# A decoder layer on one core: the clip of the weight preparation as one instruction, and mixing's inputs loaded in seven pieces

## The chip, the cores and the metric

The kernel runs on 1 core of one Trainium2 chip. The metric is the device time of one execution in microseconds (us). TensorE is called PE, VectorE DVE, ScalarE ACT, GpSimd POOL and SyncE SP, as the profile does. SP computes nothing here; it issues nearly all DMAs, in the order in which they are written, and stands still at each of its waits.

## The reference, cut to what matters

The layer takes x (16 x 128 x 256) through three parts with a layer norm behind each: a two-way RWKV mixing (`_L0_attn_ref`), a cross attention to `ctx_1024` with 16 heads, and a block of causal attention with 8 experts, two of them per token. The weights of the last block are quantised and dequantised in groups of 128 values before use:

```
w2 = w.reshape(-1, 128)
wmax, wmin = max(w2), min(w2)
scales = clip(wmax - wmin, 1e-5, None) / 15
base = clip(round(-wmin / scales), 0, 15)
wq = (clip(round(w2 / scales) + base, 0, 15) - base) * scales
```

The change is in the code that computes these lines for the attention weights and the experts' down projections.

## The kernel before, in words

The program is a list of stages (`STAGES`): prep, mix, cross, attend, route, experts, finish. Every engine has one stream of instructions that runs through the stages in order; semaphores order the engines among each other. So an engine that is done with its part of prep may start its part of mix, if what that waits for is there.

**Prep** works on 11 jobs (`NUMBERS`). A job is 128 partitions of 14 groups of 128 f32 values (`TILES` = 14, `P` = 128), 896 KB. Three buffers each of `raw`, `level`, `turned` and `stat` rotate (index j = n mod 3). For job n:

- SP loads it from `weight_jobs` into `raw` (L312).
- DVE reduces each group to its maximum and minimum (L261, L262) and computes the small numbers, 14 a partition, in eight steps that each wait for the one before (`group_steps`, L263 to L271): scale, inverse, base, and `LOW`/`HIGH`, the ends between which the rounded value is to be clipped.
- ACT rounds: 14 instructions (L372), one a group, each adding MAGIC = 1.5 x 2^23, so that f32 rounds to whole numbers.
- DVE clips groups 0 to 9 in ten instructions (L358), POOL clips groups 10 to 13 in four (L398), both between `LOW` and `HIGH` of the group.
- POOL dequantises: 14 instructions (L405), (level - MAGIC) x scale.
- PE transposes the 14 tiles into four banks (L422), ACT copies the banks to `turned` (L381), SP stores them to `numbers_d` (L317), from where later stages load them.

The order on each engine is written out: DVE does the numbers of job n+1 and then clips job n; ACT rounds job n+2 and then copies job n; POOL and PE take the jobs in turn. The numbers of job n+1 wait until POOL has dequantised job n-2, whose `stat` buffer they take (semaphore `dequantised`). SP's order: loads of jobs 0, 1, 2; then, each behind the rounding of an earlier job that frees its buffer, the loads of jobs 3 and 4; then all inputs of mixing (`load_mix_inputs`: `w_rkv`, two `x_turned`, `w_out`, `decay`, `first`, and the first `x_group`, about 6.5 MB) and of cross (`load_cross_weights`, seven DMAs, about 1 MB); then for n from 2 on: wait for the rounding of job n, load job n+3, wait for the copies of job n-2, store it.

**Mix** starts on DVE, ACT and POOL when SP has seen the last store of prep land and raises `begun` (L173), and on PE when the last bank of prep is copied and the mixing inputs are there (`mix_loads`, 16 a DMA, `LOADS` = 6 of them). PE projects (L527), ACT takes the result (L573). SP's part begins with the loads for attend (L214 to L218) and goes on with the next group of x (L186) when DVE has the variances of the group before.

**Cross** has a preparation of its own for 16 more jobs, interleaved with attention. It finds the small numbers with `group_range` and `group_bias` (L232 to L252: sums over pairs made with `tensor_reduce`, through a buffer with a gap of one, `spaced`), adds `BIAS` = base + MAGIC when rounding (L1056), clips the whole job in one instruction between MAGIC and MAGIC + 15 (L1199), and subtracts `BIAS` on POOL in two halves with the `BIAS` of each group broadcast along its 128 values (L1128).

Of the kernel before, what the change touches and what calls it, by code (L numbers as in the profile page):

```python
# [22 lines left out]
ALU = mybir.AluOpType  # L23
# [3 lines left out]
P = 128  # L27
# [14 lines left out]
TILES = 14  # L42
# [53 lines left out]
class Shared:  # L96
# [75 lines left out]

        sp.sem_inc(self.begun, 1)  # L173

    def load_mix_inputs(self, sp):
        t = self.t
        for src, dst in ((t["rkv_t"], self.w_rkv), (t["x_fwd_t"], self.x_turned[0]), (t["x_bwd_t"], self.x_turned[1]),
                         (t["out_t"], self.w_out)):
            sp.dma_start(dst[:, :, :], src.rearrange("(c p) n -> p c n", p=P)).then_inc(self.mix_loads, 16)

        sp.dma_start(self.decay[:, :], t["decay"]).then_inc(self.mix_loads, 16)
        sp.dma_start(self.first[:, :], t["first"]).then_inc(self.mix_loads, 16)
        self.load_group(sp, 0)
# [46 lines left out]
def group_range(dve, st, a, groups):  # L230

    dve.tensor_reduce(a[:, MAX, :], groups, AX.X, ALU.max)  # L232
    st.did(dve.tensor_reduce(a[:, NEG_MIN, :], groups, AX.X, ALU.min, negate=True))  # L233
# [18 lines left out]
    return dve.tensor_reduce(in_pairs(BIAS), row_pair(a, BASE, SHIFT), AX.X, ALU.add)  # L252


def group_steps(dve, st, a, groups):

    def step(ins):
        st.did(ins)
        st.wait()

    dve.tensor_reduce(a[:, MAX, :], groups, AX.X, ALU.max)  # L261
    step(dve.tensor_reduce(a[:, MIN, :], groups, AX.X, ALU.min))  # L262
    step(dve.tensor_tensor(a[:, TMP, :], a[:, MAX, :], a[:, MIN, :], ALU.subtract))  # L263
    step(dve.tensor_scalar(a[:, SCALE, :], a[:, TMP, :], 1e-5, 1.0 / LEVELS, ALU.max, ALU.mult))
    step(dve.reciprocal(a[:, INV, :], a[:, SCALE, :]))
    step(dve.scalar_tensor_tensor(out=a[:, TMP, :], in0=a[:, MIN, :], scalar=-1.0, in1=a[:, INV, :],
                                  op0=ALU.mult, op1=ALU.mult))
    step(dve.tensor_scalar(a[:, BASE, :], a[:, TMP, :], MAGIC, MAGIC, ALU.add, ALU.subtract))
    step(dve.tensor_scalar(a[:, TMP, :], a[:, BASE, :], 0.0, LEVELS, ALU.max, ALU.min))
    step(dve.tensor_scalar(a[:, LOW, :], a[:, TMP, :], -1.0, MAGIC, ALU.mult, ALU.add))  # L270
    return dve.tensor_scalar(a[:, HIGH, :], a[:, LOW, :], LEVELS, None, ALU.add)  # L271


def prep_stage(k):


# [4 lines left out]
    with ExitStack() as own:  # L281
        raw = [k.buffer(own, f"raw{j}", [TILES, P]) for j in range(3)]
        level = [k.buffer(own, f"level{j}", [TILES, P]) for j in range(3)]
        turned = [k.buffer(own, f"turned{j}", [TILES, P]) for j in range(3)]
        stat = [k.buffer(own, f"stat{j}", [8, TILES]) for j in range(3)]
    raw_in = [k.semaphore(f"raw_in{j}") for j in range(3)]
    stored = [k.semaphore(f"stored{j}") for j in range(3)]
    scale_ready = k.semaphore("scale_ready")
    rounded = k.semaphore("rounded")
    clipped = k.semaphore("clipped")  # L290
    pool_clipped = k.semaphore("pool_clipped")
# [4 lines left out]
    DVE_TILES = 10  # L296
# [12 lines left out]

    def sync(sp):  # L310
        def load(j, n):
            sp.dma_start(raw[j][:, :, :], t["weight_jobs"][bass.ds(n, 1)].rearrange(  # L312
                "o p (a b) -> (o p) a b", a=TILES)).then_inc(raw_in[j], 16)

        def store(j, n):
            sp.wait_ge(bank_read, (n + 2) * BANKS_JOB)
            sp.dma_start(k.numbers_d[bass.ds(n, 1)].rearrange("o p (a b) -> (o p) a b", a=TILES),  # L317
                         turned[j][:, :, :]).then_inc(stored[j], 16)

        def element(j, n, more=True, begin=False):  # L320

            if more:
                sp.wait_ge(rounded, n + 1)
                load(j, n + 3)
            if not begin:
                store((j + 1) % 3, n - 2)

        for j in range(3):
            load(j, j)
            sp.sem_inc(stored[j], 16)  # L330
        for n in range(2):
            element(n, n, begin=True)
        k.load_mix_inputs(sp)
        k.load_cross_weights(sp)
        with sp.Fori(0, TURNS) as i:
            for d in range(3):
                element((2 + d) % 3, 3 * i + 2 + d)
        for n in range(3 * TURNS + 2, NUMBERS):
            element(n % 3, n, more=False)
        for n in range(NUMBERS - 2, NUMBERS):  # L340
            store(n % 3, n)
        for j in range(3):
            sp.wait_ge(stored[j], 16 * (1 + len(range(j, NUMBERS, 3))))

    def vector(dve):
        st = k.steps["dve"]

        def steps_of(j, n, i):
            dve.wait_ge(raw_in[j], 16 * i + 16)
            dve.wait_ge(dequantised, n + 1)  # L350
            group_steps(dve, st, stat[j], raw[j][:, :, :]).then_inc(scale_ready, 1)

        def element(j, n, i, more):
            if more:
                steps_of((j + 1) % 3, n + 1, i + (j + 1) // 3)
            dve.wait_ge(rounded, n + 1)
            for a in range(DVE_TILES):
                last = dve.tensor_scalar(level[j][:, a, :], level[j][:, a, :], stat[j][:, LOW, a:a + 1],  # L358
                                         stat[j][:, HIGH, a:a + 1], ALU.max, ALU.min)
            last.then_inc(clipped, 1)  # L360

        dve.tensor_copy(k.ident16[:, :], k.ident).then_inc(k.s_fill, 1)
        steps_of(0, 0, 0)
        st.done(1, 8)
        in_pipeline(element, dve, st, 24)
        st.done(1, st.at)

    def scalar(act):
        def round_levels(j, n):
            act.wait_ge(scale_ready, n + 1)  # L370
            for a in range(TILES):
                last = act.activation(level[j][:, a, :], raw[j][:, a, :], ACT.Identity, bias=k.magic[:, :],  # L372
                                      scale=stat[j][:, INV, a:a + 1])
            last.then_inc(rounded, 1)

        def take_tiles(j, n, i):
            act.wait_ge(stored[j], 16 * i + 16)
# [12 lines left out]
        round_levels(1, 1)  # L390
        in_pipeline(element, act)

    def gpsimd(pool):
        def element(j, n, i, more):
            pool.wait_ge(rounded, n + 1)
            pool.sem_inc(k.s_held, 1)
            for a in range(DVE_TILES, TILES):
                last = pool.tensor_scalar(level[j][:, a, :], level[j][:, a, :], stat[j][:, LOW, a:a + 1],  # L398
                                          stat[j][:, HIGH, a:a + 1], ALU.max, ALU.min)
            last.then_inc(pool_clipped, 1)  # L400
            pool.wait_ge(clipped, n + 1)
            pool.wait_ge(pool_clipped, n + 1)
            pool.sem_inc(k.s_held, 1)
            for a in range(TILES):
                last = pool.tensor_scalar(level[j][:, a, :], level[j][:, a, :], -MAGIC,  # L405
                                          stat[j][:, SCALE, a:a + 1], ALU.add, ALU.mult)
            last.then_inc(dequantised, 1)

        pool.sem_inc(dequantised, 3)
        in_pipeline(element, pool)  # L410

    def tensor(pe):
        def element(j, n, i, more):
# [17 lines left out]
def mix_stage(k):  # L431
# [6 lines left out]
    nc, t, banks = k.nc, k.t, k.banks  # L438
    x_turned, w_rkv, w_out = k.x_turned, k.w_rkv, k.w_out
    decay, first, x_group, group_in = k.decay, k.first, k.x_group, k.group_in  # L440
    LOADS = 6
    with ExitStack() as own:
        step_decay = k.buffer(own, "step_decay", [UNITS])
        top = [k.buffer(own, f"top{p}", [GB, S + 1]) for p in range(2)]
# [47 lines left out]
    def sync(sp):  # L492
# [8 lines left out]
        k.begin(sp, "mix")  # L501
        sp.sem_inc(mix_stored, 16)
        k.load_attend_weights(sp)
        with sp.Fori(0, GROUPS - 1) as g:
            element(g, True)
        sp.wait_ge(mix_stored, 32)
# [1873 lines left out]
```

## Time and profile before

| | us |
|---|---|
| median of 3 runs | 1266.79 |
| lowest, highest | 1266.73, 1269.02 |
| profiled execution | 1267.29 |
| its span | 1265.5 |
| prep: the first raw reduction to the last copy | 8.7 to 123.2 |
| mixing's first projection read by ACT | 130.6 |
| busy on DVE, POOL, ACT, PE over the span | 977.0, 621.7, 744.9, 996.2 |

The profile shows one execution. The span is the time between its first and its last record; the execution's own time is 1.8 us longer. Instructions are shown with their start, so that a wait is the gap ahead of one. The prep stage fills the first tenth of the span.

### The profile page before, as it was taken

The numbers are of one execution on the slowest core, as the hardware profiler recorded it, in microseconds if no ns is written. First come the engines' busy times: TensorE is split into PE (matmuls) and PEld (weight loads), VectorE is DVE, ScalarE is ACT, GpSimd is POOL, SyncE is SP. The second block draws the span as 40 slices with busy tenths as digits, with TensorE's granted clock in tenths as the row PEclk, the third lists the DMA queues.
The fourth block names the chain that finished last, engine by engine and source line by source line (L and its number), as shares of the span: only waits on it lengthen the run. The fifth ranks groups of instructions, "written<-read, shape, count | busy, mean of one in ns | idle before, by whom it ended". The sixth has DMA issues, their size and how long they took to land.

```text
span 1265.5 us, 25848 instructions
## 1 busy us (share of the span) xinstructions
PE 996.2 (79%) x7366; PEld 749.1 (59%) x7367; DVE 977.0 (77%) x2276; ACT 744.9 (59%) x1882; POOL 621.7 (49%) x813
## 2 busy tenths in 40 slices
PE   0334966861699899896899999983799999999990
PEld 0323433431477777773566667652688888888880
DVE  6894799999888888874688888856576777777773
ACT  4785634432288888882455655540466666666663
POOL 3897587777244444442255555544234334333333
PEclk9755978876788999987899999996899999999995
DMA  4953200000323333322122222230112122122124
GB/s 177 402 196 139 96 1 13 20 33 17 124 90 125 136 119 112 112 77 75 34 93 99 95 95 95 92 121 17 31 39 41 33 39 36 36 41 35 37 31 141
DMA packets 56028, 105.83 MB, mean 84 GB/s; under 512 B 10080, under 2 KB 41824, under 8 KB 55472
## 3 DMA queue, kind: packets, MB, share of 16 engines
q1 hardware_dynamic: 47872, 92.52, 20.9%
q0 software_dynamic: 8112, 12.78, 5.6%
q8 instruction: 20, 0.33, 0.1%
q14 instruction: 24, 0.20, 0.0%
HBM read 70.96 MB, written 34.32 MB: 83 GB/s over the span
## 4 chain that ended last, share of the span: by engine, by line
PE 50%; DVE 24%; issue 7%; POOL 4%; ACT 3%; DMA 2%; DVEq 0%; ACTq 0%; POOLq 0%; SPq 0%
PE banks L2014 15%; PE banks L2024 10%; DVE mix_sums L679 4%; PE banks L1380 4%; PE banks L1423 3%; PE banks L1402 3%; DVE whole_stat L232 2%; DVE whole_stat L233 2%; PE banks L1415 2%; DVE peak L1159 2%; PE banks L1372 2%; DVE carry L669 2%; DVE probs L1162 2%; DVE carry L666 2%; PE banks L913 1%
## 5 line engine op out<-in xcount | busy, mean ns | idle before, releaser
L2097 DVE SCALAR_TENSOR_TENSOR expert_gate<-banks,expert_steps,expert_chunk 128x128 f32<-128x128 f32 x546 | 166.1, 346 | 96.9 <-ACT expert_chunk L2059 95.0
L2014 PE MATMUL banks<-expert_parts,levels 128*128 128x128 bf16 x3276 | 228.9, 220 | 8.3 <-issue 5.5
L2014 PEld LDWEIGHTS banks<-expert_parts,levels 128*128 x3276 | 202.7, 98 | 49.1 <-issue 21.4
L2024 PE MATMUL banks<-down,up 128*128 x546 | 176.2, 406 | 0.0
L2059 ACT COPY expert_chunk<-banks 128x256 f32<-128x256 f32 x273 | 101.5, 372 | 103.4 <-PE banks L2014 103.4
L2154 POOL DMA_INDIRECT summed_d<-expert_y,expert_target x39 | 62.4, 1601 | 180.3 <-ACT expert_y L2069 170.8
L527 PE MATMUL banks<-x_turned,w_rkv 128*128 128x512 f32 (+1 forms) x192 | 100.8, 685 | 39.4 <-DVE weight L660 38.8
L2063 ACT ACTIVATE silu<-expert_gate,expert_steps 128x128 f32<-128x128 f32 x273 | 110.7, 406 | 16.2 <-DVE expert_gate L2097 16.0
L422 PE MATMUL banks<-consts,level 128*128 128x128 f32 x154 | 35.6, 424 | 87.1 <-POOL level L405 87.1
L1128 POOL TENSOR_TENSOR whole<-whole_level,whole_stat 128x896 bf16<-128x896 f32 x32 | 53.2, 1685 | 102.3 <-DVE whole_level L1199 102.3
L2104 DVE SCALAR_TENSOR_TENSOR up<-expert_gate,expert_steps,silu 128x128 f32<-128x128 f32 x273 | 94.0, 344 | 9.3 <-ACT silu L2063 9.3
L527 PEld LDWEIGHTS banks<-x_turned,w_rkv 128*128 128x128 f32 x192 | 41.7, 223 | 96.1 <-issue 95.0
L1056 ACT ACTIVATE whole_level<-whole_raw,whole_stat 128x128 f32<-128x128 f32 x224 | 91.2, 486 | 0.6 <-DVE whole_stat L252 0.6
L422 PEld LDWEIGHTS banks<-consts,level 128*128 128x128 f32 x154 | 31.3, 226 | 90.7 <-POOL level L405 43.6
L2024 PEld LDWEIGHTS banks<-down,up 128*128 128x128 f32 x546 | 83.0, 191 | 0.4
L372 ACT ACTIVATE level<-raw,magic,stat 128x128 f32<-128x128 f32 x154 | 60.3, 479 | 19.3 <-DVE stat L271 19.3
L1595 POOL TENSOR_TENSOR att_probs<-att_probs,att_share 128x1024 f32<-128x1024 f32 x16 | 30.3, 1896 | 72.4 <-DVE att_share L1712 72.4
L951 PE MATMUL banks<-v_ones,probs_t 128*128 128x17 f32 x512 | 61.2, 262 | 0.1
L951 PEld LDWEIGHTS banks<-v_ones,probs_t 128*128 128x128 f32 x512 | 59.7, 192 | 0.2 <-ACT probs_t L1041 0.2
L578 ACT ACTIVATE weight<-weight 128x1024 f32<-128x1024 f32 x16 | 16.9, 1057 | 71.9 <-DVE weight L660 71.9
L1380 PE MATMUL banks<-attend_w,xn_t 128*128 128x512 f32 x128 | 58.8, 602 | 0.0
L1423 PE MATMUL banks<-attend_w,o_turn 128*128 128x256 f32 x256 | 58.1, 380 | 0.5 <-ACT logits L1526 0.5
(237 smaller groups left out, 2535.7 us busy)
## 6 DMA issues: line engine op xcount, KB each, us to landing
whole_raw<-in_weight_jobs SPq DMA_DIRECT2D x16, 896.0 KB, 4.9
raw<-in_weight_jobs SPq DMA_DIRECT2D x11, 896.0 KB, 5.5
numbers_d<-turned SPq DMA_DIRECT2D x11, 896.0 KB, 5.0
levels_d<-whole_t SPq DMA_DIRECT2D x16, 448.0 KB, 2.7
levels<-levels_d SPq DMA_DIRECT2D x16, 448.0 KB, 3.4
down<-numbers_d SPq DMA_DIRECT2D x16, 448.0 KB, 4.2
normed_d<-normed_parts SPq DMA_DIRECT2D x16, 192.0 KB, 1.9
attend_w<-numbers_d SPq DMA_DIRECT2D x3, 896.0 KB, 6.7
```

The costliest lines, as they stand in the source:

```text
L422: last = pe.transpose(banks[:, 4 * (j % 2) + b, a * P:(a + 1) * P], level[j][:, 4 * b + a, :], k.ident)
L527: last = pe.matmul(banks[:, 3 * (u % 2) + m, :], w_rkv[:, kc, col:col + P], x_turned[d][:, kc, bass.ds(g * GT, GT)], start=(kc == 0), stop ...
L951: last = pe.matmul(banks[:, HEADS, head * (XK + 1):(head + 1) * (XK + 1)], probs_t[h][:, 4 * m + a, :], v_ones[j][:, head, :], start=True, ...
L1056: last = act.activation(level[j][:, a, :], raw[j][:, a, :], ACT.Identity, bias=stat[j][:, BIAS, a:a + 1], scale=stat[j][:, INV, a:a + 1])
L1380: last = pe.matmul(banks[:, Q + m, :], xn_t[:, c, :], w_qkv[:, c, 512 * m:512 * m + 512], start=(c == 0), stop=(c == DC - 1))
L1423: last = pe.matmul(banks[:, TURN, 0:D], o_turn[:, h, :], w_o[:, h, :], start=(h == 0), stop=(h == QH - 1))
L2014: last = pe.matmul(banks[:, at, (m * DC + c) * ROWS:(m * DC + c + 1) * ROWS], levels[:, bass.ds(expert * (2 * JOB) + (m * JOB + (f * DC + ...
L2024: last = pe.matmul(banks[:, Y + j, 0:D], up[j][:, f, :], down[:, bass.ds(expert * JOB + f * D, D)], start=(f == 0), stop=(f == FC - 1))
L2059: act.copy(chunk[slot(j, f)][:, :, :], halves(at)[:, :, 0, :]).then_inc(chunk_ready, 1)
L2063: act.activation(silu[slot(j, f)][:, :], gate[slot(j, f)][:, 0, :], ACT.Silu, scale=steps[j][:, 0, 0, f:f + 1]).then_inc(silu_ready, 1)
L2097: last = dve.scalar_tensor_tensor(out=gate[slot(j, f)][:, m, :], in0=halves(at)[:, m, 1, :], scalar=steps[j][:, m, 1, f:f + 1], in1=chunk[ ...
L2104: dve.scalar_tensor_tensor(out=up[j][:, f, :], in0=gate[slot(j, f)][:, 1, :], scalar=steps[j][:, 1, 0, f:f + 1], in1=silu[slot(j, f)][:, : ...
```

## The change

Clip and small numbers in prep take the form that cross has. DVE uses `group_range` and `group_bias` (six steps and two reductions) with a buffer `prep_spaced`; `SHIFT` is filled with MAGIC once for each of the three `stat` buffers. ACT adds `BIAS` of the group in place of MAGIC, in the same 14 instructions. DVE clips the whole job (128 x 1792) in one instruction. POOL clips nothing; once DVE has clipped, it subtracts the broadcast `BIAS` over the whole job, waits for that, and multiplies by the broadcast `SCALE`.

SP's part of prep is written out for all jobs. Mixing's inputs are cut in seven pieces (the halves of `w_rkv`, of the two `x_turned`, and the rest together), one behind the raw load of each of the iterations 1 to 7. They count nine DMAs. The seven DMAs of the cross weights are issued in mix, behind those for attend.

```diff
-    def load_mix_inputs(self, sp):
+    def load_mix_half(self, sp, src, dst, c):
+        sp.dma_start(dst[:, c, :], src[c * P:(c + 1) * P, :]).then_inc(self.mix_loads, 16)
+
+    def load_mix_small(self, sp):
         t = self.t
...
+        sp.dma_start(self.w_out[:, :, :], t["out_t"].rearrange("(c p) n -> p c n", p=P)).then_inc(self.mix_loads, 16)
         sp.dma_start(self.decay[:, :], t["decay"]).then_inc(self.mix_loads, 16)
         sp.dma_start(self.first[:, :], t["first"]).then_inc(self.mix_loads, 16)
         self.load_group(sp, 0)
...
-        for n in range(2):
-            element(n, n, begin=True)
-        k.load_mix_inputs(sp)
-        k.load_cross_weights(sp)
-        with sp.Fori(0, TURNS) as i:
...
+        for n in range(NUMBERS):
+            if n + 3 < NUMBERS:
+                sp.wait_ge(rounded, n + 1)
+                load(n % 3, n + 3)
+            if n == 1:
+                k.load_mix_half(sp, t["rkv_t"], k.w_rkv, 0)
...
+            if n == 5:
+                k.load_mix_small(sp)
...
+            if n == 7:
+                k.load_mix_half(sp, t["x_bwd_t"], k.x_turned[1], 1)
+            if n >= 2:
+                store((n - 2) % 3, n - 2)
...
-            group_steps(dve, st, stat[j], raw[j][:, :, :]).then_inc(scale_ready, 1)
+            group_range(dve, st, stat[j], raw[j][:, :, :])
+            group_bias(dve, st, stat[j], spaced).then_inc(scale_ready, 1)
...
-            for a in range(DVE_TILES):
-                last = dve.tensor_scalar(level[j][:, a, :], level[j][:, a, :], stat[j][:, LOW, a:a + 1],
-                                         stat[j][:, HIGH, a:a + 1], ALU.max, ALU.min)
-            last.then_inc(clipped, 1)
+            dve.tensor_scalar(level[j][:, :, :], level[j][:, :, :], MAGIC, MAGIC + LEVELS, ALU.max,
+                              ALU.min).then_inc(clipped, 1)
...
-                last = act.activation(level[j][:, a, :], raw[j][:, a, :], ACT.Identity, bias=k.magic[:, :],
+                last = act.activation(level[j][:, a, :], raw[j][:, a, :], ACT.Identity, bias=stat[j][:, BIAS, a:a + 1],
...
-            pool.wait_ge(rounded, n + 1)
+            pool.wait_ge(clipped, n + 1)
             pool.sem_inc(k.s_held, 1)
-            for a in range(DVE_TILES, TILES):
...
-            pool.wait_ge(clipped, n + 1)
-            pool.wait_ge(pool_clipped, n + 1)
+            st.did(pool.tensor_tensor(level[j][:, :, :], level[j][:, :, :], wide(stat[j][:, BIAS, :], P), ALU.subtract))
+            st.wait()
             pool.sem_inc(k.s_held, 1)
-            for a in range(TILES):
-                last = pool.tensor_scalar(level[j][:, a, :], level[j][:, a, :], -MAGIC,
-                                          stat[j][:, SCALE, a:a + 1], ALU.add, ALU.mult)
-            last.then_inc(dequantised, 1)
+            pool.tensor_tensor(level[j][:, :, :], level[j][:, :, :], wide(stat[j][:, SCALE, :], P),
+                               ALU.mult).then_inc(dequantised, 1)
...
-    LOADS = 6
+    LOADS = 9
...
         k.load_attend_weights(sp)
+        k.load_cross_weights(sp)
         with sp.Fori(0, GROUPS - 1) as g:
```

## Rows read from the trace of the kernel before

**Rows 1.** The page, busy time: us (share of the span) xinstructions.

```profile
PE 996.2 (79%) x7366; PEld 749.1 (59%) x7367; DVE 977.0 (77%) x2276; ACT 744.9 (59%) x1882; POOL 621.7 (49%) x813
```

**Rows 2.** Table by stretches: engines' busy time, granted clock, DMA share, GB/s.

```profile
30.00:40.00 10.00, 4.63 (x21) 4.24 (x22) 9.68 (x26) 7.79 (x20) 9.52 (x20) 1.00 1.01 416
40.00:50.00 10.00, 4.60 (x22) 4.21 (x21) 9.72 (x27) 8.56 (x23) 9.61 (x21) 0.76 1.04 371
```

**Rows 3.** Timeline (start, duration, engine, line, xcount), one steady job of prep.

```profile
85.50 3.33 POOL L398 TENSOR_SCALAR level<-level,stat 128x128 f32<-128x128 f32 x4
86.36 5.50 ACT L372 ACTIVATE level<-raw,magic,stat 128x128 f32<-128x128 f32 x14 [1.37 <-DVE stat L271]
...
89.15 4.92 POOL L405 TENSOR_SCALAR level<-level,stat 128x128 f32<-128x128 f32 x14 [0.32 <-DVE level L358]
...
91.76 1.79 ACT L381 COPY turned<-banks 128x512 f32<-128x512 f32 x4
...
94.06 3.33 POOL L398 TENSOR_SCALAR level<-level,stat 128x128 f32<-128x128 f32 x4
```

**Rows 4.** Timeline, the first job.

```profile
8.68 2.02 DVE L261 TENSOR_REDUCE stat<-raw 128x14 f32<-128x1792 f32 x1 [4.40 <-DMA raw<-in_weight_jobs]
...
12.66 0.17 DVE L263 TENSOR_TENSOR stat<-stat 128x14 f32<-128x14 f32 x1
...
14.19 0.17 DVE L271 TENSOR_SCALAR stat<-stat 128x14 f32<-128x14 f32 x1
...
15.76 10.87 ACT L372 ACTIVATE level<-raw,magic,stat 128x128 f32<-128x128 f32 x28
...
21.29 2.85 DVE L358 TENSOR_SCALAR level<-level,stat 128x128 f32<-128x128 f32 x10 [1.12 <-ACT level L372]
...
25.02 4.92 POOL L405 TENSOR_SCALAR level<-level,stat 128x128 f32<-128x128 f32 x14 [0.20 <-POOL level L398]
```

**Rows 5.** Timeline, the raw load of job 5 and who waits for it.

```profile
48.08 0.35 SPq L312 DMA_DIRECT2D raw<-in_weight_jobs  x1
...
54.99 2.02 DVE L261 TENSOR_REDUCE stat<-raw 128x14 f32<-128x1792 f32 x1 [4.38 <-DMA raw<-in_weight_jobs]
```

**Rows 6.** Timeline, the last job on POOL and mixing's first read on ACT.

```profile
114.51 4.92 POOL L405 TENSOR_SCALAR level<-level,stat 128x128 f32<-128x128 f32 x14 [0.20 <-issue]
...
130.60 0.60 ACT L573 ACTIVATE gate<-banks 128x512 f32<-128x512 f32 x1 [3.55 <-PE banks L527]
```

**Rows 7.** Timeline, cross: clip, subtraction, first and last of six small steps.

```profile
392.25 1.09 DVE L1199 TENSOR_SCALAR whole_level<-whole_level 128x1792 f32<-128x1792 f32 x1
...
393.51 3.33 POOL L1128 TENSOR_TENSOR whole<-whole_level,whole_stat 128x896 bf16<-128x896 f32 x2 [6.41 <-DVE whole_level L1199]
...
395.74 0.17 DVE L247 TENSOR_REDUCE whole_spaced<-whole_stat 128x14 f32<-128x28 f32 x1
...
396.85 0.18 DVE L252 TENSOR_REDUCE whole_stat<-whole_stat 128x14 f32<-128x28 f32 x1
```

**Rows 8.** Groups of POOL by shape: busy us, mean ns of one.

```profile
L615 POOL TENSOR_TENSOR mix_sums<-weight,carry 128x512 f32<-128x512 f32 x32 | 40.0, 1270 | 15.5 <-DVE carry L669 15.5
...
L1110 POOL TENSOR_TENSOR spread<-k_t,consts 128x512 f32<-128x512 f32 x32 | 32.6, 1039 | 10.1 <-ACT q_t L1030 9.4
L1595 POOL TENSOR_TENSOR att_probs<-att_probs,att_share 128x1024 f32<-128x1024 f32 x16 | 30.3, 1896 | 72.4 <-DVE att_share L1712 72.4
...
L1117 POOL TENSOR_TENSOR x_bias<-x_in,bias_rows 128x256 f32<-128x256 f32 x16 | 11.6, 725 | 2.5 <-SPq L173 2.5
```

**Rows 9.** Timeline of DVE and of POOL in the route stage.

```profile
873.83 6.57 DVE L1905 TENSOR_TENSOR row_hit<-lane,consts 128x2048 f32<-128x2048 f32 x2
...
874.97 3.28 POOL L1838 TENSOR_TENSOR block_hit<-block_hit,shares 128x624 f32<-128x624 f32 x1
...
881.46 1.27 POOL L1838 TENSOR_TENSOR block_hit<-block_hit,shares 128x624 f32<-128x624 f32 x1
```

**Rows 10.** The page, DMA issues: count, KB each, median us from issue to landing.

```profile
raw<-in_weight_jobs SPq DMA_DIRECT2D x11, 896.0 KB, 5.5
```

More of the change, by code:

```diff
@@ L173, in begin @@
         sp.sem_inc(self.begun, 1)
-    def load_mix_inputs(self, sp):
+    def load_mix_half(self, sp, src, dst, c):
+        sp.dma_start(dst[:, c, :], src[c * P:(c + 1) * P, :]).then_inc(self.mix_loads, 16)
+    def load_mix_small(self, sp):
         t = self.t
-        for src, dst in ((t["rkv_t"], self.w_rkv), (t["x_fwd_t"], self.x_turned[0]), (t["x_bwd_t"], self.x_turned[1]),
-                         (t["out_t"], self.w_out)):
-            sp.dma_start(dst[:, :, :], src.rearrange("(c p) n -> p c n", p=P)).then_inc(self.mix_loads, 16)
+        sp.dma_start(self.w_out[:, :, :], t["out_t"].rearrange("(c p) n -> p c n", p=P)).then_inc(self.mix_loads, 16)
         sp.dma_start(self.decay[:, :], t["decay"]).then_inc(self.mix_loads, 16)
@@ L252, in group_bias @@
     return dve.tensor_reduce(in_pairs(BIAS), row_pair(a, BASE, SHIFT), AX.X, ALU.add)
[L255 to L271, printed above, removed]
 def prep_stage(k):
@@ L285, in prep_stage @@
         stat = [k.buffer(own, f"stat{j}", [8, TILES]) for j in range(3)]
+        spaced = k.buffer(own, "prep_spaced", [TILES // 2, 3])
     raw_in = [k.semaphore(f"raw_in{j}") for j in range(3)]
@@ L290, in prep_stage @@
     clipped = k.semaphore("clipped")
-    pool_clipped = k.semaphore("pool_clipped")
     tiles_turned = k.semaphore("tiles_turned")
@@ L318, in store @@
                          turned[j][:, :, :]).then_inc(stored[j], 16)
[L320 to L326, printed above, removed]
         for j in range(3):
@@ L330, in sync @@
             sp.sem_inc(stored[j], 16)
-        for n in range(2):
-            element(n, n, begin=True)
-        k.load_mix_inputs(sp)
-        k.load_cross_weights(sp)
-        with sp.Fori(0, TURNS) as i:
[L336 to L339, printed above, removed]
+        for n in range(NUMBERS):
[4 more added lines that the diff above has]
+                k.load_mix_half(sp, t["rkv_t"], k.w_rkv, 0)
+            if n == 2:
+                k.load_mix_half(sp, t["rkv_t"], k.w_rkv, 1)
+            if n == 3:
+                k.load_mix_half(sp, t["x_fwd_t"], k.x_turned[0], 0)
+            if n == 4:
+                k.load_mix_half(sp, t["x_fwd_t"], k.x_turned[0], 1)
+            if n == 5:
+                k.load_mix_small(sp)
+            if n == 6:
+                k.load_mix_half(sp, t["x_bwd_t"], k.x_turned[1], 0)
+            if n == 7:
+                k.load_mix_half(sp, t["x_bwd_t"], k.x_turned[1], 1)
+            if n >= 2:
+                store((n - 2) % 3, n - 2)
         for n in range(NUMBERS - 2, NUMBERS):
@@ L356, in element @@
             dve.wait_ge(rounded, n + 1)
-            for a in range(DVE_TILES):
-                last = dve.tensor_scalar(level[j][:, a, :], level[j][:, a, :], stat[j][:, LOW, a:a + 1],
-                                         stat[j][:, HIGH, a:a + 1], ALU.max, ALU.min)
-            last.then_inc(clipped, 1)
+            dve.tensor_scalar(level[j][:, :, :], level[j][:, :, :], MAGIC, MAGIC + LEVELS, ALU.max,
+                              ALU.min).then_inc(clipped, 1)
         dve.tensor_copy(k.ident16[:, :], k.ident).then_inc(k.s_fill, 1)
+        for j in range(3):
+            st.did(dve.memset(stat[j][:, SHIFT, :], MAGIC))
         steps_of(0, 0, 0)
-        st.done(1, 8)
-        in_pipeline(element, dve, st, 24)
+        st.done(1, st.at)
+        in_pipeline(element, dve, st, 18)
         st.done(1, st.at)
@@ L393, in gpsimd @@
     def gpsimd(pool):
+        st = k.steps["pool"]
         def element(j, n, i, more):
-            pool.wait_ge(rounded, n + 1)
+            pool.wait_ge(clipped, n + 1)
             pool.sem_inc(k.s_held, 1)
-            for a in range(DVE_TILES, TILES):
-                last = pool.tensor_scalar(level[j][:, a, :], level[j][:, a, :], stat[j][:, LOW, a:a + 1],
-                                          stat[j][:, HIGH, a:a + 1], ALU.max, ALU.min)
-            last.then_inc(pool_clipped, 1)
-            pool.wait_ge(clipped, n + 1)
-            pool.wait_ge(pool_clipped, n + 1)
+            st.did(pool.tensor_tensor(level[j][:, :, :], level[j][:, :, :], wide(stat[j][:, BIAS, :], P), ALU.subtract))
+            st.wait()
             pool.sem_inc(k.s_held, 1)
-            for a in range(TILES):
-                last = pool.tensor_scalar(level[j][:, a, :], level[j][:, a, :], -MAGIC,
-                                          stat[j][:, SCALE, a:a + 1], ALU.add, ALU.mult)
-            last.then_inc(dequantised, 1)
+            pool.tensor_tensor(level[j][:, :, :], level[j][:, :, :], wide(stat[j][:, SCALE, :], P),
+                               ALU.mult).then_inc(dequantised, 1)
         pool.sem_inc(dequantised, 3)
-        in_pipeline(element, pool)
+        in_pipeline(element, pool, st, 3)
+        st.done(1, st.at)
     def tensor(pe):
```

1 line of the change is left out of this document (removed).

## The prediction

> **What bounds the kernel now.** I read the page first: no engine is busy all the time; the highest is TensorE with 79% [rows 1]. The change touches only the preparation stage (the first tenth of the span) and what mixing finds loaded, so the shares of the whole say little; I went on to the table by stretches and the timeline there. From 30 to 50 us POOL and DVE are over 95% busy and the DMA engines are full at 416 and 371 GB/s [rows 2].
>
> One steady job on the timeline: POOL starts its four clip instructions at 85.50, its fourteen dequantising ones at 89.15, and the next job's clips at 94.06 [rows 3]. That is a pitch of 8.55 us, of which 8.25 (3.33 + 4.92) is POOL at work. ACT rounds in 5.50 and copies in 1.79, 7.2 together with their overlap [rows 3], and is the second longest. POOL bounds the stage. From the end of job 0 on POOL (25.02 + 4.92 = 29.94, [rows 4]) to the end of job 10 (114.51 + 4.92 = 119.43, [rows 6]) are 89.49 us: ten pitches of 8.55 and 4.0 more. Those 4.0 are one stall: the raw load for job 5 is issued only at 48.08, because SP stood behind the issues of mixing's and cross's inputs; DVE waits 4.38 for it [rows 5], and POOL behind DVE.
>
> Behind job 10 come its transposes and copies, then mixing's first projection, whose result starts ACT at 130.60 [rows 6]. This tail is the same code after the change, so the time follows the end of job 10 on POOL one to one.
>
> **The change, part by part.**
>
> *Small numbers.* Before, eight DVE steps from 12.66 to 14.36, 1.70 us [rows 4]. After, the six steps that cross already uses, 395.74 to 397.03: 1.29 [rows 7], and these ran while POOL was inside a tensor_tensor, so POOL does not stretch them. With the two reductions (8.68 to 12.66: 3.98, [rows 4]) a job's numbers cost 5.27. Three memsets of constants fall into DVE's wait for the first raw job: nothing.
>
> *Clip.* Ten DVE instructions and four POOL ones become one DVE instruction over 1792 columns: 1.09 in cross [rows 7].
>
> *POOL.* The fourteen short instructions become two tensor_tensors over 1792 columns with a broadcast operand. Rows of that kind: 512 columns 1.039, 1024 columns 1.896 [rows 8], slope 1.674 ns a column; 896 columns took 3.33 for two [rows 7], on the same line. So 1792 columns take 1.896 + 768 x 0.001674 = 3.18 each. The second waits for the first by semaphore, with a held count between; POOL's wait for its own clips cost 0.20 (the idle time at 25.02, [rows 4]), and I take that.
>
> *The new wait.* POOL no longer works on a job while DVE clips it; everything POOL does for the job, and behind it the transposes and ACT's copies, waits for DVE's clip. From its end at 393.34 to POOL's start at 393.51: 0.17 [rows 7]. Where does the clip fall? DVE computes the numbers of job n+1 (5.27) and then clips job n; POOL meanwhile works on job n-1 for 0.17 + 3.18 + 0.20 + 3.18 = 6.73. So the clip is issued inside POOL's second pass. No row shows a two-column-a-cycle DVE instruction (1792 columns in 1.09 is over one a cycle) against a long POOL one. The nearest: at 873.83 DVE has two instructions of 2048 columns with two SBUF inputs, 6.57 together; POOL's instructions of 624 columns beside them take 3.28 each, against 1.27 for the last one once DVE's have gone [rows 9]. The two engines alternate by whole instructions. The bounds: clip free (no alternation), or it waits to the end of POOL's pass and then runs. I take the latter, nearest to these rows, with the clip's own run at 1792 / 1.92 GHz = 0.93, called 0.97 for its end.
>
> The Trainium skill, page SBUF — State Buffer, section "Who interferes with whom", says that a DVE instruction in a two-port mode and a GpSimd instruction hold a shared port pair for the whole instruction and that the later one blocks fully, and that tensor_reduce never does. This agrees with the alternation in [rows 9] and with the sum as taken; were it otherwise here, the first rival below would be the sum.
>
> *Pitch.* From one POOL end to the next: clip after release 0.97, wait 0.17, pass 3.18, wait 0.20, pass 3.18 = 7.70. ACT needs 7.2, and its rounding starts when the numbers are there, 5.3 after the clip, so it is 0.4 from being the bound. DVE: 5.27 + 1.2 blocked + 0.97 fills the pitch, but only because it waits.
>
> *Start.* Numbers ready 0.41 earlier, rounding starts at 15.35 instead of 15.76 and takes 5.44 (half of 10.87); clip 0.09 behind it, 20.87 (before 21.29); done 21.96; POOL 22.13 + 3.18 + 0.20 + 3.18 = 28.69 [rows 4, 7]. Before 29.94.
>
> *Loads.* Seven pieces replace SP's burst: two halves of w_rkv (0.79 MB each), four of x_turned (1.05 MB each), and w_out with decay, first and x_group (1.05 MB), one a job. A raw load (0.92 MB) stands ahead of each piece, a store (0.92 MB) behind it: 2.9 MB a pitch at most, which at 7.70 is 375 GB/s, under the 371 to 416 of a full queue [rows 2] by little. What this may delay is the raw load: it is issued when ACT has rounded job n, and job n+3's numbers start on DVE 12.3 later (rounding of job n ends 5.3 + 5.5 = 10.8 after the clip of job n-2; the numbers of job n+3 start after the clip of job n+1, three pitches or 23.1 behind it). Between issue and landing a median of 5.5 lies [rows 10]. So 6.8 of slack, and the stall of 4.0 goes. Nothing else is late in its place: a store has two more pitches before ACT wants its buffer. The seven cross DMAs go behind mixing's `begin` and the attend loads; the next thing on SP behind them is the load of mixing's second group, which waits for DVE's variances of a whole first group anyway, and their weights are wanted only after mixing: nothing. PE's wait counts nine loads instead of six, all issued by job 7: nothing.
>
> *Sum.* Job 10 ends on POOL at 28.69 + 10 x 7.70 = 105.7 instead of 119.43: 13.7 less. By terms: start 1.25, pitch 10 x 0.85 = 8.5, stall 4.0. The profiled execution took 1267.29 (span 1265.5 and 1.8 around it): 1253.6. The runs' median is 0.5 below it, so 1253.1.
>
> **Rivals.**
>
> *No blocking, ACT bounds* (10%). If the clip ran beside POOL's pass, POOL would need 6.73 and ACT's 7.2 with a wait of 0.15 would be the pitch: 7.35, another 3.5 less: 1249.6. For: nothing here shows exactly this pair. Against: [rows 9].
>
> *The stall stays* (10%). If mixed reads and writes ran at 300 GB/s, 2.9 MB would take 9.6, 1.9 over the pitch for six pieces, 11.4, less the slack of 6.8: 4.6 lost. 1257.7. For: the queue is 94% full for seven jobs. Against: [rows 2] held 371 to 416 with small rows among them. The Trainium skill, DMA: Bandwidth & Descriptors, section "Measured", gives 341 GB/s for a DMA of 1 MB; by it the lag is 0.8 a piece and stays inside the slack.
>
> *The slower side: POOL's passes at the rate of two full operands* (4%). Two full inputs take 0.725 at 256 columns and 1.270 at 512 [rows 8]: 2.1 ns a column, and 1792 columns 3.96. The pitch is then 2 x 3.96 + 0.20 + 0.97 + 0.17 = 9.26; job 0 ends at 30.25, job 10 at 122.85, 3.4 later than now: 1270.2. It decides from a pass of 3.8 on, where the lost pitch eats what the start and the stall give. Against: the subtracting pass of cross has the same operands and lies on the broadcast line.
>
> *It does nothing* (1%): the tail waits for something else. ACT starts at 130.60 right behind PE's projection [rows 6], which is behind job 10's copies, so no.
>
> **How the numbers follow.** The forecast has 75%, its own range 1250 to 1257: passes of 3.1 to 3.35 (with 22 of them, -1.8 to +3.7), and 1 to 2 us by how fast TensorE's granted clock is for the first projections. The two near rivals bring it to 1248.5 to 1259. A measurement of this kernel tells about 0.2% (2.5 us) from no change. Faster 0.94, within 0.02, slower 0.04.
>
> **What would show it.** On POOL two instructions a job of 3.2, 0.2 apart, at a pitch of 7.7; the DVE clip shown as 2 us or more, ending about 0.97 after POOL's pass; no DVE wait on a raw load; ACT idle 0.4 a job; mixing's first ACT instruction at about 116.9. Wrong would be: clips of 1.09 beside a running pass, passes of 3.8, or DVE waiting for raw jobs 5 to 10.

## The result and the profile after

Four runs of each kernel: before 1267.9 us (1266.73 to 1272.66), after 1251.3 (1250.14 to 1253.71). The ratio is 0.986, interval 0.9836 to 0.9884: 1.4% faster. The median forecast was 1253.1. The profiled execution, one of the four, took 1250.84 (span 1249.0); 1253.6 was forecast for it. Timed again later, the changed kernel is 1.2 to 1.3% faster (see Repeats).

The page's busy times, to be read beside [rows 1]:

```profile
PE 995.4 (80%) x7366; PEld 748.7 (60%) x7367; DVE 964.6 (77%) x2158; ACT 745.8 (60%) x1882; POOL 605.0 (48%) x637
```

POOL lost 16.7 us of work and DVE 12.4, and the span lost 16.5. That these agree is chance, since busy time includes waits and all stages are in it: the next views show where the time comes from.

The timeline of the first job after, which answers to [rows 4] (start, duration, engine, line, tiles and shapes, count, and in brackets the idle time before and what ended it):

```profile
12.66 0.18 DVE L247 TENSOR_REDUCE prep_spaced<-stat 128x14 f32<-128x28 f32 x1
...
13.78 0.18 DVE L252 TENSOR_REDUCE stat<-stat 128x14 f32<-128x28 f32 x1
...
15.36 10.88 ACT L356 ACTIVATE level<-raw,stat 128x128 f32<-128x128 f32 x28
...
20.88 1.09 DVE L341 TENSOR_SCALAR level<-level 128x1792 f32<-128x1792 f32 x1 [1.52 <-ACT level L356]
...
22.25 3.17 POOL L383 TENSOR_TENSOR level<-level,stat 128x1792 f32<-128x1792 f32 x1 [21.76 <-DVE level L341]
...
25.61 3.18 POOL L386 TENSOR_TENSOR level<-level,stat 128x1792 f32<-128x1792 f32 x1 [0.18 <-POOL level L383]
```

The first clip has POOL idle beside it: 1.09. Job 0 leaves POOL at 25.61 + 3.18 = 28.79. The steady pattern, which answers to [rows 3]:

```profile
44.99 2.01 DVE L232 TENSOR_REDUCE stat<-raw 128x14 f32<-128x1792 f32 x1
...
48.69 3.18 POOL L386 TENSOR_TENSOR level<-level,stat 128x1792 f32<-128x1792 f32 x1 [0.18 <-POOL level L383]
...
50.17 2.65 DVE L341 TENSOR_SCALAR level<-level 128x1792 f32<-128x1792 f32 x1
50.29 5.50 ACT L356 ACTIVATE level<-raw,stat 128x128 f32<-128x128 f32 x14 [0.47 <-DVE stat L252]
...
52.74 2.00 DVE L232 TENSOR_REDUCE stat<-raw 128x14 f32<-128x1792 f32 x1
53.00 3.18 POOL L383 TENSOR_TENSOR level<-level,stat 128x1792 f32<-128x1792 f32 x1 [1.13 <-DVE level L341]
```

The row to learn from is the clip at 50.17. It is the instruction that took 1.09 in the first job, and it shows 2.65. It starts inside POOL's pass (48.69 + 3.18 = 51.87) and ends at 52.82, 0.95 behind it. POOL meanwhile waits for it, and starts 0.18 later. DVE looks busy all the time and is not: 1.6 of the 2.65 are a wait that the profile books as work. Job 5, for whose raw data DVE waited 4.38 in [rows 5], has its numbers computed from 44.99 on and waits for nothing; no job but the first does.

The end, which answers to [rows 6]:

```profile
94.26 1.23 DVE L341 TENSOR_SCALAR level<-level 128x1792 f32<-128x1792 f32 x1 [3.08 <-ACT level L356]
94.72 3.81 POOL L386 TENSOR_TENSOR level<-level,stat 128x1792 f32<-128x1792 f32 x1 [0.18 <-POOL level L383]
98.49 3.17 POOL L383 TENSOR_TENSOR level<-level,stat 128x1792 f32<-128x1792 f32 x1
...
101.84 3.18 POOL L386 TENSOR_TENSOR level<-level,stat 128x1792 f32<-128x1792 f32 x1 [0.18 <-POOL level L383]
...
116.47 0.60 ACT L555 ACTIVATE gate<-banks 128x512 f32<-128x512 f32 x1 [3.85 <-PE banks L509]
```

Here the order is turned round. No numbers are left to compute, so DVE clips the last job as soon as ACT has rounded it, at 94.26, ahead of POOL's pass, and it is POOL that is held: 3.81 instead of 3.18. Job 10 leaves POOL at 105.02 (before 119.44), 14.4 earlier, and mixing's first read on ACT comes at 116.47 (before 130.60), 14.1 earlier.

The table by stretches, for [rows 2] (PE, PEld, DVE, ACT and POOL busy with counts, granted clock, DMA share, GB/s):

```profile
30.00:40.00 10.00, 5.42 (x25) 4.62 (x23) 9.63 (x11) 9.27 (x25) 8.69 (x3) 1.00 0.81 255
40.00:50.00 10.00, 3.25 (x14) 2.85 (x14) 9.62 (x15) 9.51 (x24) 8.43 (x4) 1.00 1.00 350
50.00:60.00 10.00, 3.65 (x16) 3.26 (x17) 9.76 (x12) 9.15 (x24) 8.23 (x3) 0.93 1.00 384
60.00:70.00 10.00, 5.49 (x27) 5.10 (x26) 9.79 (x11) 9.52 (x26) 8.02 (x3) 0.50 1.04 379
```

POOL has gone from 9.5 of 10 to 8.0 to 8.7. The burst of 416 GB/s is gone: the queue moves 255 GB/s in the first of these stretches and 350 to 384 in the other three. The page's DMA issues give for the raw jobs a median of 7.3 us to landing, where [rows 10] had 5.5:

```profile
raw<-in_weight_jobs SPq DMA_DIRECT2D x11, 896.0 KB, 7.3
```

### The profile page after: what moved, and what is told of

Its sections match the earlier page's. It is cut to its first block, busy times and chain, and to the rows that moved or that the text cites. A ratio compares the mean times of both kernels' runs of the same rounds, so it can differ in the third digit from the quotient of the medians.

```text
span 1249.0 us, 25514 instructions
## 1 busy us (share of the span) xinstructions
PE 995.4 (80%) x7366; PEld 748.7 (60%) x7367; DVE 964.6 (77%) x2158; ACT 745.8 (60%) x1882; POOL 605.0 (48%) x637
## 4 chain that ended last, share of the span: by engine, by line
PE 51%; DVE 28%; issue 9%; POOL 4%; ACT 3%; DMA 3%; DVEq 0%; SPq 0%; POOLq 0%; ACTq 0%
PE banks L1996 15%; PE banks L2006 10%; PE banks L1362 4%; DVE mix_sums L661 4%; PE banks L1405 4%; PE banks L1384 3%; PE banks L1354 2%; DVE whole_stat L232 2%; DVE whole_stat L233 2%; DVE peak L1141 2%; PE banks L1397 2%; DVE carry L651 2%; DVE carry L648 2%; DVE probs L1144 2%; DVE stat L232 2%
## 5 line engine op out<-in xcount | busy, mean ns | idle before, releaser
L356 ACT ACTIVATE level<-raw,stat 128x128 f32<-128x128 f32 x154 | 60.4, 480 | 5.0 <-DVE stat L252 4.9
```

## The experiments

The theory: the pitch is POOL's two passes plus a clip that the pass in front of it holds back; the stall is SP's burst and goes with it alone. The rivals: the clip isn't held and ACT bounds the stage; the loads or the arithmetic alone bring most of it. "Prep end" is where job 10 leaves POOL. It is the number to compare: of one code it repeats within 0.3 us, the whole time does not, as will be seen. "Pitch" is the time from one job's end on POOL to the next, and a ratio is to the kernel before timed beside the run, whose medians were 1270.8 to 1271.3.

**Loads alone** (the arithmetic of before, with SP's new order), e1_loads_only:

```diff
-        k.load_mix_inputs(sp)
-        k.load_cross_weights(sp)
...
+            if n == 1:
+                k.load_mix_half(sp, t["rkv_t"], k.w_rkv, 0)
...
```

> The kernel before with SP's part of the change alone: seven pieces behind the raw loads, nine counted loads, cross weights in mixing. Clips, small numbers and POOL's fourteen instructions as before. Theory (POOL is the bound at 8.55 us a job, and the burst of loads costs one stall of 4.0): job 10 ends on POOL at about 115.4 instead of 119.43, no DVE wait on a raw load behind the first, and the time is 4.0 below the kernel before. Rival (the stall is hidden again by a wait that takes its place, or pieces delay every raw load): time within 1.5 us of the kernel before, with DVE waiting on raw loads.

Its last job on the timeline:

```profile
110.42 4.93 POOL L408 TENSOR_SCALAR level<-level,stat 128x128 f32<-128x128 f32 x14 [0.20 <-issue]
```

Prep end 115.34, 4.1 earlier than before, pitch 8.55, no wait for a raw job but the first. Time 1264.9, ratio 0.9956 (0.9934 to 0.9978): 5.9 below the kernel before, of which prep gives 4.1; the rest is within what equal code differs by behind prep.

**Arithmetic alone** (after, with SP's order of before), e2_burst_loads:

```diff
-            if n == 1:
-                k.load_mix_half(sp, t["rkv_t"], k.w_rkv, 0)
...
+        k.load_mix_inputs(sp)
+        k.load_cross_weights(sp)
```

> The changed kernel with SP's order of before: all of mixing's and cross's inputs in one burst behind the raw load of job 4. Theory (SP is held until about 47.7 by the burst, whatever the compute does, so the raw load of job 5 lands near 54.6; the faster compute wants it at 45.0): DVE waits about 9.6, POOL's end of job 10 comes about 8 later than in the changed kernel, the time is near 1259.4. Rival (the stall is a fixed term of 4.0, as in the sum of the prediction): 1255.3. Second rival (the loads' place does not matter at this pitch): 1251.3.

The late load and the two engines behind it:

```profile
47.98 0.35 SPq L292 DMA_DIRECT2D raw<-in_weight_jobs  x1
...
54.74 2.02 DVE L232 TENSOR_REDUCE stat<-raw 128x14 f32<-128x1792 f32 x1 [9.43 <-DMA raw<-in_weight_jobs]
...
61.20 3.18 POOL L380 TENSOR_TENSOR level<-level,stat 128x1792 f32<-128x1792 f32 x1 [9.09 <-DVE level L338]
```

SP gets through its burst at 47.98, as before the change (48.08, [rows 5]): the arithmetic has no part in that. But the faster jobs want the load earlier, so the wait is 9.43 and no longer 4.38. Prep end 113.22: 6.2 earlier than before, 8.2 later than after. Time 1261.9, ratio 0.9942 (0.9921 to 0.9963). The two halves give 4.1 and 6.2 alone and 14.4 together: 4.1 belong to neither. The times expected beforehand for this run and the next two were counted from 1251.3 for the changed kernel; timed again it took 1253.8 and 1254.1, so a time some 2.5 above such a figure is no miss of the mechanism.

**A clip that can't be held**, e3_one_port_clip. ACT rounds into rows of 257 columns, and DVE reads 7 rows of 256 there and writes 1792 dense columns: so the source's outermost count is 7 and the destination is one row of 1792.

```diff
+        apart = [k.buffer(own, f"apart{j}", [TILES // 2, 2 * P + 1]) for j in range(3)]
-            dve.tensor_scalar(level[j][:, :, :], level[j][:, :, :], MAGIC, MAGIC + LEVELS, ALU.max,
-                              ALU.min).then_inc(clipped, 1)
+            dve.tensor_scalar(level[j][:, :, :].rearrange("p (a o) b -> p a (o b)", o=2), apart[j][:, :, 0:2 * P], MAGIC,
+                              MAGIC + LEVELS, ALU.max, ALU.min).then_inc(clipped, 1)
...
-                last = act.activation(level[j][:, a, :], raw[j][:, a, :], ACT.Identity, bias=stat[j][:, BIAS, a:a + 1],
...
+                last = act.activation(apart[j][:, a // 2, a % 2 * P:(a % 2 + 1) * P], raw[j][:, a, :], ACT.Identity,
```

> The changed kernel, but ACT rounds into a buffer whose 256-column rows lie 257 apart, and DVE's one clip reads that and writes the dense buffer. The clip is as many columns in one instruction, with one SBUF input; its two access patterns differ, as in the small steps that POOL did not stretch. Theory (the clip runs two columns a cycle and for that alternates with POOL's passes by whole instructions; at one column a cycle it does not): the clip takes about 1.97 with POOL's pass running beside it, POOL's passes stay 3.18, ACT (7.2 and a wait) becomes the bound, pitch about 7.3 instead of 7.67, time about 3.7 below the changed kernel: 1247.6. Rival (the clip waits for something else than the engine's ports, or any DVE instruction alternates with POOL): clip 3.4 or more, pitch 8.6, time 9 above the changed kernel: 1260.

The steady pattern on its timeline:

```profile
62.38 3.18 POOL L387 TENSOR_TENSOR level<-level,stat 128x1792 f32<-128x1792 f32 x1 [0.18 <-POOL level L384]
63.94 2.01 DVE L342 TENSOR_SCALAR level<-apart 128x1792 f32<-128x1792 f32 x1
64.06 5.50 ACT L357 ACTIVATE apart<-raw,stat 128x128 f32<-128x128 f32 x14
65.86 2.01 DVE L232 TENSOR_REDUCE stat<-raw 128x14 f32<-128x1792 f32 x1
66.13 3.19 POOL L384 TENSOR_TENSOR level<-level,stat 128x1792 f32<-128x1792 f32 x1 [0.57 <-DVE level L342]
```

The clip takes 2.01, where it took 1.09 with POOL idle, and takes it beside POOL's pass: it ends at 65.95, 0.39 behind the pass's end at 65.56, and the pass keeps its 3.18. The slower instruction is done sooner: the held clip ended 0.95 behind the pass. The pitch falls to 7.11, prep ends at 100.52, 4.5 earlier than after. Time 1250.4, ratio 0.9847 (0.981 to 0.9885). In its repeat the table by stretches says what bounds the stage now:

```profile
60.00:90.00 30.00, 14.48 (x63) 12.48 (x62) 26.20 (x36) 30.00 (x77) 27.00 (x9) 0.50 0.80 320
```

ACT is busy 30.00 of 30: its copies and roundings follow each other without a gap. The Trainium skill, VectorE: DVE Perf Modes, section "Mode 2×_2P — use both read ports for one tensor", says that a single-source instruction gets two columns a cycle if the outermost non-unit dimension is even, or odd and the same for source and destination. The rows agree: 1.09 for 1792 on 1792, and 2.01 for an odd 7 on 1792.

**The small numbers in plain steps**, e4_plain_numbers: after, with six dense steps instead of the pair sums. The first has two SBUF inputs:

```diff
-            group_bias(dve, st, stat[j], spaced).then_inc(scale_ready, 1)
+            plain_bias(dve, st, stat[j]).then_inc(scale_ready, 1)
...
+    step(dve.tensor_tensor(a[:, TMP, :], a[:, MAX, :], a[:, NEG_MIN, :], ALU.add))
```

> The changed kernel with the small numbers as six plain steps (tensor_tensor and tensor_scalar on dense 14-column rows) in place of the sums over pairs. Same count of steps, same values. Theory (plain steps alternate with POOL by whole instructions, and POOL's instructions are now 3.18 long): the first step is issued 0.27 into POOL's second pass and waits to its end, so the numbers end about 8.1 after the last clip and the next clip at 9.2; pitch about 9.2 instead of 7.67, time 14 to 15 above the changed kernel, near 1266. Rival (a plain step is stretched by 0.15 at most, as beside POOL's short instructions in the kernel before): pitch 7.7, time as the changed kernel, 1251.3.

```profile
61.54 3.18 POOL L401 TENSOR_TENSOR level<-level,stat 128x1792 f32<-128x1792 f32 x1 [0.18 <-POOL level L398]
61.89 2.86 DVE L262 TENSOR_TENSOR stat<-stat 128x14 f32<-128x14 f32 x1
64.79 0.17 DVE L263 TENSOR_SCALAR stat<-stat 128x14 f32<-128x14 f32 x1
...
65.77 1.09 DVE L356 TENSOR_SCALAR level<-level 128x1792 f32<-128x1792 f32 x1
67.04 3.18 POOL L398 TENSOR_TENSOR level<-level,stat 128x1792 f32<-128x1792 f32 x1 [2.31 <-DVE level L356]
```

An addition of 14 columns takes 2.86: it ends at 64.75, 0.03 behind POOL's pass. The clip behind it is late, and POOL idles 2.31 a job. Pitch 8.86 (9.2 expected), prep end 116.67, time 1265.6, ratio 0.9965 (0.9943 to 0.9987). Taking the pair sums out of the changed kernel costs 11.7 us of prep, by another road than the 0.41 that I had given them. The other five steps run behind the pass, so this run tells of the two-input step alone.

**POOL's two steps in one instruction a tile**, e7_fused_pool: fourteen tensor_scalars with bias and scale as two per-partition numbers.

```diff
-            st.did(pool.tensor_tensor(level[j][:, :, :], level[j][:, :, :], wide(stat[j][:, BIAS, :], P), ALU.subtract))
...
+                last = pool.tensor_scalar(level[j][:, a, :], level[j][:, a, :], stat[j][:, BIAS, a:a + 1],
+                                          stat[j][:, SCALE, a:a + 1], ALU.subtract, ALU.mult)
```

> The changed kernel with POOL's two passes as fourteen tensor_scalars, one a group, each subtracting the group's BIAS and multiplying by its SCALE, both per partition. It asks what made POOL's four clips of before take 0.78 each while its fourteen dequantising ones took 0.35. If it is two per-partition numbers in one instruction: 14 x 0.78 = 10.9 a job, pitch about 11.3, time 35 above the changed kernel, 1285. If it is max and min: 14 x 0.35 = 4.9, POOL is no longer the bound, DVE's clip no longer waits 1.5 behind a long pass, ACT bounds at 7.1 to 7.3, and the time is 3 to 4 below the changed kernel.

One group by line and engine: count, least, median and most ns of one, from when to when.

```profile
L384 POOL TENSOR_SCALAR level<-level,stat x154: 782/787/1824, 22.2 to 149.8; 128x128 f32<-128x128 f32 x154
```

0.78 each, against 0.35 (4.92 / 14, [rows 3]) with one number and a constant. So in [rows 3] the four clips of 3.33 were dear for their two numbers, not for max and min. Pitch 11.7, where 11.3 was expected: from the second job on one POOL instruction a job, the one beside DVE's clip, takes 1.5 to 1.8 instead of 0.78. The clip itself takes 1.08 to 1.27 here, so it is mostly POOL that is held: behind an instruction of 0.78 the fast clip lost at most 0.2, behind a pass of 3.18 it lost 1.6. Prep end 150.5, 45.5 behind after: 5.1 in the first job (11.63 against 6.54) and 40.4 in the ten that follow. DVE waits some 5.4 a job for POOL, so nothing hides it. One execution took 1304.4, beside 1271.1 of the kernel before; 1285 was expected. Prep gives 45.5 where 35 was expected, and the stretch behind prep is 1151.6, longer than any in the table below.

**Cross weights back in prep**, e8_cross_in_prep:

```diff
+            if n == 8:
+                k.load_cross_weights(sp)
...
-        k.load_cross_weights(sp)
```

> The changed kernel with the seven DMAs of the cross weights back in prep, issued in SP's iteration 8 behind the last raw load. Theory (their place is worth nothing once they are behind the raw loads; 1 MB in an idle queue): prep's last POOL pass ends at 105.0 as in the changed kernel, no raw wait, time within 1.5 of it apart from TensorE's clock later. Rival (they delay the store of job 6 and with it ACT's buffer): ACT's copies of job 9 wait on a store, prep ends 1 to 3 later.

Prep end 104.98, as after. The w_q load, whose issue as part of the burst had taken SP 5.48, is issued in 0.79. For prep it is worth nothing where these seven loads stand, once it is not in the burst. The whole was executed once, in 1256.0, and its 1149.1 behind prep lie among those of the changed kernel below.

**Repeats.** The one-port kernel left prep 4.5 earlier, and its ratio was lower by only 0.0013, 1.6 us. So both were run again, and before too.

> The changed kernel unaltered, beside the next one on the same chip. Theory (14 us of the gain are made by the end of prep, the rest is how TensorE's granted clock falls at the first and last steps of cross and attend): 0.986 to 0.989 of the kernel before; mixing's first read on ACT at 116 to 118, and from there to the end of the span 1132 to 1136, where the kernel before has 1134.9.

> The kernel with the one-port clip again, timed in five rounds beside the changed kernel. In its first profile prep ended 4.5 earlier than in the changed kernel, but 4.9 went at the end of cross, where TensorE was granted 0.52 for ten us. Theory (that loss is of the one execution and belongs to no code): prep's last POOL pass ends at 100.5 again, cross ends without the long last step, and the median is 3 to 5 below the changed kernel's. Rival (the earlier start falls into a worse clock every time): prep at 100.5 again, the last step of cross long again, and the median level with the changed kernel's within 1.5.

> The kernel before unaltered, for a second profile of it. Open: the medians say 16.6 and 17.0 less, prep's last POOL pass is 14.4 earlier; the other 2.4 lie behind prep. Theory (they are TensorE's granted clock in this or that execution): prep's last POOL instruction ends at 119.4 again, and what follows it differs from the first profile's 1146.1 by up to 4 in either direction. Rival (the kernel before has a fixed loss behind prep, which the change takes away): 1146 to 1149 again, and more than the changed kernel's in every pair of profiles of one chip.

> The changed kernel unaltered, a third profile, on the same chip as the one of the kernel before. Its first two had 1143.9 and 1148.6 behind the last POOL pass of prep, at 105.0 both times. Theory: 105.0 again, and a time behind it anywhere from 1143 to 1150, decided by whether TensorE is granted half or full speed in the last steps of cross and the first of attend. Rival: below the kernel before's of this chip by 2.4.

> The changed kernel once more in five rounds, as the partner of the next one. Expected: prep's last POOL pass ends at 105.0, median within 2 of 1254.

> The one-port clip once more in five rounds beside the changed kernel. Its prep is 4.7 shorter in every profile; in the timing before, the medians lay only 2.1 apart, with runs from 1248.6 to 1253.7. Theory (the 4.7 arrive in the mean, and TensorE's clock spreads single executions over 5 us): a median 3 to 6 below its partner's here, 3 to 5 over both timings. Rival (half of the 4.7 is given back behind prep each time): 2 again or less.

Of each profile: the prep end, cross (the start of ACT's first copy of a transposed input to the start of DVE's last result), attend from there up to its first normalised tile, and all that lies behind the prep end.

| kernel | prep end | cross | attend's first | behind prep |
|---|---|---|---|---|
| before | 119.44 | 250.61 | 53.31 | 1146.1 |
| before again | 119.22 | 250.66 | 53.24 | 1150.3 |
| after | 105.02 | 248.65 | 51.96 | 1143.9 |
| after, e5 | 105.06 | 254.22 | 53.38 | 1148.6 |
| after, e10 | 105.04 | 254.22 | 53.44 | 1150.8 |
| after, e11 | 105.00 | 249.79 | 52.66 | 1147.0 |
| one port, e3 | 100.52 | 254.75 | 53.39 | 1149.5 |
| one port, e6 | 100.24 | 250.05 | 52.59 | 1146.5 |
| one port, e12 | 100.22 | 250.25 | 52.44 | 1146.5 |

The same code behind prep took 1143.9 to 1150.8, and the one stage of cross between 248.65 and 254.75 (mixing 204.2 to 204.4 each time). Nor is it cross alone. The two profiles of the kernel before differ by 4.2 behind prep and agree up to route, whose first `row_hit` starts at 873.83 and 873.62; from 862 to 895 TensorE was granted 0.66 and 0.60. Nor has the kernel before a loss of its own behind prep: on one chip it had 1150.3 there, and the changed kernel (e10) 1150.8.

From the prep end to mixing's first read on ACT the changed kernel took 11.45, 9.28, 11.63 and 11.33. TensorE, busy nearly all of it with the same 27 matmuls, was granted 0.64 in the first, 0.85 in the second and 0.63 in the third. So two of what was expected of e5 did not come: the read at 116 to 118 came at 114.34, and the 1132 to 1136 from there to the end were 1139.3.

The end of cross in one good and one bad execution of the kernel after, the table by stretches of after:

```profile
555.00:565.00 10.00, 9.02 (x70) 7.53 (x68) 4.50 (x9) 5.96 (x11) 3.88 (x3) 0.90 0.16 61
565.00:575.00 10.00, 2.40 (x9) 1.33 (x9) 3.98 (x15) 0.78 (x3) 1.64 (x3) 0.61 0.59 154
```

and of e10:

```profile
555.00:565.00 10.00, 8.09 (x50) 6.75 (x47) 4.85 (x9) 5.49 (x10) 3.88 (x3) 0.79 0.16 61
565.00:575.00 10.00, 7.07 (x30) 5.42 (x28) 2.19 (x7) 1.92 (x5) 0.35 (x1) 0.50 0.35 110
```

In the first TensorE is granted 0.90 of full speed (2.4 GHz) in the mean and runs 70 matmuls; in the second 0.79, and it runs 50, and the rest follow at 0.50, which is the lower level, 1.2 GHz. What came before the fall was the same code in both: TensorE was busy 9.52 of the ten us before, in either.

Timed again on two occasions, side by side: after 1254.1 and 1253.8, ratios 0.9869 (0.9848 to 0.9889) and 0.9876 (0.9844 to 0.9908); one port 1252.0 and 1249.9, ratios 0.9858 (0.9836 to 0.988) and 0.9851 (0.9824 to 0.9877). With these ten runs of each, the medians are 1253.9 and 1250.7, the means 1254.3 (deviation of one run 2.8) and 1251.1 (2.1): 3.2 less for one port, 0.9 to 5.5. The first occasion alone gave 2.1, where 3 to 5 was expected, the second 3.9. (With the first four runs of each, which were not timed beside each other, it is 2.7.) Of the 4.8 of prep most seems to arrive, but the interval includes everything from a fifth of it to all of it. One port is the best version here.

## Why the prediction was right

**The pitch.** 7.70 forecast. Nine job ends from 28.79 to 90.23 (job 8) are eight pitches of 7.68. Passes 3.17 to 3.19 but for one (forecast 3.18, from 1024 columns in [rows 8]), wait between them 0.18 (0.20), clip 0.95 behind the pass (0.97). The prediction has DVE blocked 1.2 a job; its own terms leave 1.46 (7.70 - 5.27 - 0.97), and the trace shows about 1.6, which is in no term of the sum. The forecast's choice, that the two engines hold each other by whole instructions, was taken from one place in route [rows 9]; the clip's 2.65, the 14 columns of e4 that took 2.86, and e3, where clip and pass run beside each other, show it in this stage. The Trainium skill, SBUF — State Buffer, section "Who interferes with whom", has the three cases, two-port mode, two SBUF inputs and neither, and the 2.65, the 2.86 and the 2.01 are one of each.

**The start and the stall.** Job 0 leaves POOL at 28.79 (28.69 forecast). No raw job is waited for after the first. The landing of the raw loads was mis-sized: 7.3 in the median and 8.8 at most, not 5.5. It had 12.3 of room (from the issue at 32.72 to the numbers at 44.99 for job 5), so 3.5 of it remain at worst, where the prediction left 6.8.

**The last jobs.** 105.7 forecast, 105.02 measured. Job 9 takes 8.30 and job 10 6.50, together 14.8, not 15.4, which the prediction took for the last two as for all. The last clip is no longer behind a set of numbers and slips in front of POOL's pass.

**The terms.** 1.25 + 8.5 + 4.0 = 13.75 came out as 14.4 and is right as a sum; it is wrong as a list of what each part brings. The stall is 4.0 only at a pitch of 8.55; with the new arithmetic the burst costs 8.2 (e2 against after). Small numbers were entered at 0.41 for the start; undone, they cost 11.7 (e4), since their two-input step would wait for each pass. A term that was costed against the kernel before is not what its undoing shows.

**The rivals.** "No blocking" fell with the clip of 2.65 and with e3, which had to be built to make it true: its pitch was 7.11, near the 7.35 given. "The stall stays" fell: no wait, in stretches that moved up to 384 GB/s. The slower side fell: passes of 3.18, not 3.96. Had the arithmetic come without the new order of loads, the stall would have stayed, and 1261.9 would have been the time.

**The tail.** "One to one" held to mixing's first read within 0.3 us between the profiles of before and after, and that is luck: e5 reached this read 2.1 sooner with the same prep end. It holds only on the average. The 16.5 that the profiled spans differ by are 14.4 of prep and 2.1 behind it. Cross gave 2.0 (250.61 to 248.65) and the first of attend 1.3 (53.31 to 51.96), and the stretches before and behind these took 1.2 back. E5 and e10 don't have those 2.1. I gave 1 to 2 us to the clock, and only at the first projections. There it is 2.35 at most (9.28 to 11.63); the whole behind prep differs by up to 6.9 in the table, and in the stretches compared above the slower profile had the lower granted clock. So the nearness of 1251.3 to the forecast is in part luck too: timed again, the changed kernel took 1253.8 and 1254.1, and the kernel before 1270.8 to 1271.3, not the 1266.8 that the sum started from. The difference is what held, 13.7 forecast against 14.4 in prep and 16.6, 17.0 and 17.5 between the medians. The 0.2% that I called the measurement's limit was too small: the intervals reach 0.2 to 0.3% to each side, in the repeats too. What makes the clock fall in one execution and not in another was not settled.

## What to carry to other kernels

Beside long POOL instructions, look first at which DVE instructions POOL holds: here a clip at about half the rate was done sooner than the fast one (e3), and an addition of 14 columns with two SBUF inputs waited 2.7 of a pass of 3.18 (e4). Beside POOL instructions of 0.78 the fast clip lost at most 0.2 (e7). What a part is worth depends on the others: a late transfer costs more once the work in front of it is faster, so undo parts from the changed kernel too before you drop one. Compare the end of the changed stage first (here within 0.3 us), and whole times only over many runs.

## What was not expected

- POOL's tensor_scalar of 128 columns costs 0.78 with two per-partition numbers and 0.35 with one and a constant (e7, [rows 3]).
- The hold works in both directions: POOL's pass behind a clip of 1.23 took 3.81.
- One load of the burst took SP 5.48 to issue, and the burst ended at 48 whatever the arithmetic did (e2); the same load outside the burst took 0.79 (e8). That it is the queued bytes which slow the issue is likely and was not tested by itself.
